# A three-phase sequence kernel on one core: start and middle reordered, and the first projections formed from high and low parts

## What is computed

```python
a = tanh(x @ WA.T); b = x @ WB.T                  # 16 states
h[t] = a[t] * h[t-1] + b[t]
g = sigmoid(x @ Wg.T + bg); dx = x @ WD.T + bD
x = layernorm(x + (h @ WC.T) * g + dx * (1 - g))
```

```python
w = x @ router_w + router_b;  topv, topi = top_k(w, 512)
sel = sort(topi[:, :511]);  x_sel, pos, w_sel, mask = rows of these tokens
hn = rmsnorm(x_sel, ln1)
q = rope(hn @ wq); k = rope(hn @ wk); v = hn @ wv     # 16 heads of 16
o = softmax(q k^T / 4 + mask) v @ wo;  x1 = x_sel + o
x2 = x1 + gelu(rmsnorm(x1, ln2) @ w1) @ w2
out = x with its chosen rows replaced by x2 * w_sel, other rows as they are; then layernorm(x + out)
```

## Time and profile before

| | |
|---|---|
| median of 3 runs | 514.93 us (514.45 to 515.61) |
| profiled execution | 513.3 us, of it span 511.4 us |
| busy in the span | PE 457.1, DVE 393.8, ACT 290.8, POOL 173.4 us |
| loop, 38 to 200 us | PE busy 149.65, DVE 137.21, ACT 84.44, POOL 104.42 of 162 us |
| passage, 240 to 256 us | PE 13.91, DVE 5.49, ACT 13.11 of 16 us |
| attention, 290 to 307 us | PE 17.00, DVE 16.51, ACT 15.86 of 17 us |

### The profile page before, as it was taken

One profiled execution on the slowest core, in us unless ns is written; L12 is line 12 of the kernel. 1 busy time (PEld: TensorE's weight loads), 2 busy tenths in 40 slices (PEclk: granted clock), 3 DMA queues, 4 the chain that ended last, 5 costly groups with the idle time before them and its releaser, 6 DMA issues.

```text
span 511.4 us, 10221 instructions
## 1 busy us (share of the span) xinstructions
PE 457.1 (89%) x3533; PEld 336.6 (66%) x3533; DVE 393.8 (77%) x1213; ACT 290.8 (57%) x614; POOL 173.4 (34%) x210
## 2 busy tenths in 40 slices
PE   7698999997999877998997999998998999998970
PEld 5587888776888633666674666665886666674860
DVE  4777898799788788787279999978667999966250
ACT  2435656553464532033888999954577999962200
POOL 9146667755775750373234000001000000000532
PEclk9899999999999999799999999998999999999995
DMA  8613342252222120167661000000000000000110
GB/s 244 221 43 84 107 141 83 82 155 94 83 83 83 42 84 0 39 200 240 210 191 30 3 2 3 2 2 1 0 1 2 2 1 2 3 2 1 35 37 11
DMA packets 29370, 33.89 MB, mean 66 GB/s; under 512 B 5860, under 2 KB 24968, under 8 KB 29320
## 3 DMA queue, kind: packets, MB, share of 16 engines
q1 hardware_dynamic: 23088, 24.78, 15.0%
q0 software_dynamic: 3520, 8.40, 5.5%
q10 hardware_dynamic: 2712, 0.06, 0.3%
HBM read 19.59 MB, written 13.63 MB: 65 GB/s over the span
## 4 chain that ended last, share of the span: by engine, by line
PE 46%; DVE 12%; POOL 9%; issue 7%; ACT 6%; POOLq 1%; DVEq 0%; ACTq 0%
PE ps L942 11%; PE ps L957 7%; PE ps L929 6%; PE ps L1032 4%; POOL arena L503 3%; PE ps L1009 3%; PE ps L879 3%; PE ps L666 2%; PE ps L898 2%; PE ps L781 2%; POOL r L512 2%; PE ps L905 1%; ACT arena L1252 1%; PE ps L1015 1%; POOL h_parts L562 1%
## 5 line engine op out<-in xcount | busy, mean ns | idle before, releaser
L1252 ACT ACTIVATE arena<-arena,nmax 128x511 f32<-128x511 f32 x128 | 91.5, 719 | 5.4 <-DVE nmax L1695 5.3
L1695 DVE CUSTOM_DVE_ANT_0 arena<-ps,nmask 128x511 f32<-128x511 f32 x128 | 84.8, 683 | 0.2 <-DVE nmask L1643 0.2
L942 PE MATMUL ps<-ident,arena 128*128 128x128 f32 x512 | 78.6, 276 | 3.7 <-ACT big L407 2.4
L942 PEld LDWEIGHTS ps<-ident,arena 128*128 128x128 f32 x512 | 58.7, 140 | 25.4 <-ACT arena L1252 15.0
L700 PE MATMUL ps<-wgd_hi,x_hi 128*128 128x512 f32 x128 | 51.9, 406 | 0.0
L702 PE MATMUL ps<-wgd_hi,x_lo 128*128 128x512 f32 x128 | 50.8, 397 | 0.0
L701 PE MATMUL ps<-wgd_lo,x_hi 128*128 128x512 f32 x128 | 50.6, 395 | 0.0
L929 PE MATMUL ps<-arena 96*128 96x512 bf16 x128 | 48.5, 385 | 1.9 <-DVE nmask L1643 1.1
L407 DVE COPY big<-ps 128x512 f32<-128x512 f32 x64 | 44.0, 688 | 5.0 <-PE ps L942 3.8
L503 POOL TENSOR_TENSOR arena<-arena 128x512 f32<-128x512 f32 x32 | 41.2, 1290 | 12.6 <-DVE arena L1360 11.1
L407 ACT COPY big<-ps 128x512 f32<-128x512 f32 x64 | 36.9, 576 | 8.3 <-PE ps L957 6.4
(11 more groups left out here) (250 smaller groups left out, 1041.3 us busy)
## 6 DMA issues: line engine op xcount, KB each, us to landing
arena<-in_L_attn_x SPq DMA_DIRECT2D x16, 512.0 KB, 4.6
out<-ob_sb SPq DMA_DIRECT2D x16, 512.0 KB, 3.2
w_sb<-in_L_ffn_w SPq DMA_DIRECT2D x2, 1024.0 KB, 10.7
mt_scratch<-nmask SPq DMA_DIRECT2D x8, 256.0 KB, 2.8
mt_scratch<-big SPq DMA_DIRECT2D x8, 256.0 KB, 4.6
big<-in_L_attn_Wg SPq DMA_DIRECT2D x1, 256.0 KB, 4.4
big<-in_L_attn_WD SPq DMA_DIRECT2D x1, 256.0 KB, 4.8
wqk<-in_L_ffn_wq SPq DMA_DIRECT2D x1, 256.0 KB, 7.7
```

The costliest lines, as they stand in the source:

```text
L942: mm = pe.transpose(ps[:, 2 + u % 2, k * P:(k + 1) * P], pr[u % 4][:, k * P:(k + 1) * P], ident[:, :])
L1252: act.activation(pr[u % 4][:, 0:K - 1], sm[u % 4][:, 0:K - 1], ACT.Exp, bias=nmax[:, c, h:h + 1], scale=-1.0, accum_out=rsum[:, c, h:h + 1 ...
L1695: dve.tensor_tensor_reduce(sm[u % 4][:, 0:K - 1], ps[:, S_BANKS[u % AHEAD], 0:K - 1], nmask[b][:, c, 0:K - 1], 1.0, 3.4e38, ALU.add, ALU.m ...
```

## The change

What it does, by parts:

- **Start.** PE begins with 9 fills of 512 columns on a zeroed tile as soon as that is there, and gets 12 more fills of 256 columns than before between its turns. POOL writes the constant hi_rep (an iota of 4096 elements) as its sixth step and no longer after the other constants. DVE makes wc_r before the first scan, and PE turns wc before the recurrence inputs and the second half of group 1 between group 0's input products and its state products.
- **Loop.** wq, wk and wv are multiplied by their gains in rounds 2 and 4 and rounded in rounds 3 and 5 on ACT; POOL subtracts the rounded from the full weights in rounds 4 and 6; `positions` moves from POOL's round 6 to 7.
- **Passage.** The copy of the turned x_sel is rounded (hnT_hi), DVE subtracts to get the rest (`rest_of_first`, first_lo), and each projection is made of three fp32r products instead of one f32 product. The picks of sequence 1 are made in one run of 32 products. DVE takes the odd mask tiles of sequence 1, and the mask's columns are turned one step earlier. The fills before `turn_split` are gone.
- **Attention 0** takes the banks in another order; ACT rounds w1 inside it, in turns 1 and 2.

```diff
@@ start @@
+            pe.wait_ge(bias_zeroed, 1)
+            zero_bits = bias_row.bitcast(BF16)
...
+            fill_zero(9)
             pe.wait_ge(ident_ready, 2)
...
+            fill_ident(8)
             transposes(0, 1)
+            fill_ident(4)
...
-            pe.wait_ge(split_ready, KD)
-            recurrence_inputs(0)
+            fill_ident(4)
             pe.wait_ge(split_ready, KD + 1)
...
+            recurrence_inputs(0)
+            transposes(1, 0)
             pe.wait_ge(split_ready, 2 * KD + 1)
             for G in range(NGB):
                 if G == 0:
-                    gates(G, 0)
+                    gate_inputs(G, 0)
+                    transposes(1, 1)
+                    state_products(G, 0)
@@ POOL, loop @@
+            def rest_of_weights(k):
+                pool.wait_ge(gain_ready, 2 * k + 3)
+                pool.tensor_tensor(wqk_lo[:, k, :], wqk[:, k, :], wqk_hi[:, k, :].bitcast(F32), ALU.subtract)
+                pool.tensor_tensor(wv_lo[:, k, :], wv_sb[:, k, :], wv_hi[:, k, :].bitcast(F32),
+                                   ALU.subtract).then_inc(w_lo_ready, 1)
+                pool.wait_ge(w_lo_ready, k + 1)
...
-                if G == 6:
+                if G in (4, 6):
+                    rest_of_weights(G // 2 - 2)
+                if G == 7:
                     positions()
@@ ACT, loop @@
                     gate(G, 1)
+                if G == 1:
+                    act.wait_ge(w2_loaded, 16 * (7 + 2 * HG))
+                    act.mul(q_gain[:, :], ln_col[:, 0, :], -(HD ** -0.5)).then_inc(gain_ready, 1)
+                    act.wait_ge(gain_ready, 1)
+                if G in (2, 4):
+                    scale_weights(G // 2 - 1)
+                if G in (3, 5):
+                    round_weights(G // 2 - 1)
@@ PE, passage @@
+            def project_high(b, c):
...
+                for o, hi, lo in outputs(c):
+                    for k in range(KD):
+                        for w in (hi, lo):
+                            pe.matmul(o, hnT_hi[:, k, c * P:(c + 1) * P], w[:, k, :],
+                                      start=(k == 0 and w is hi), stop=False)
+            def project_rest(b, c):
+                pe.wait_ge(hnT1_lo_ready, b * C + c + 1)
+                for (o, hi, _), signal in zip(outputs(c), (qk_done, v_done)):
+                    for k in range(KD):
+                        mm = pe.matmul(o, first_lo[:, k, c * P:(c + 1) * P], hi[:, k, :], start=False, stop=(k == KD - 1))
...
-            project(0, range(1))
+            project_high(0, 0)
+            pick_all(1)
+            project_rest(0, 0)
...
-            pe.wait_ge(v_ready[1], 2)
-            fill(7, 10)
@@ DVE, passage @@
-            angles(0)
             slots(1)
             one_hots(1)
+            rest_of_first(0, 0)
+            rest_of_first(0, 1)
+            factors(0)
+            angles(0)
+            rows(1)
...
+            odd_mask_rows()
             for c in range(C):
                 copy_turned(0, c)
                 if c < 2:
                     parts(0, 2 + c)
                     value(1, 2 + c)
-            copy_mask()
+                elif c == 2:
+                    copy_mask()
@@ ACT, attention 0 @@
+                        if b == 0 and u == 3 and hg in (1, 2):
+                            high_of_w1(hg - 1)
```

More of the change, by code:

```diff
@@ L55 @@
 AHEAD = 4
[L56 removed]
+S_BANKS = ((6, 7, 0, 1), (0, 1, 6, 7))
 M_BANKS = (4, 6, 5, 7)
[L58 removed]
 LAG = 7
@@ L747, in _ @@
             mm.then_inc(w_turned, 1)
-            for c in range(KD):
-                transposes(1, c)
+            recurrence_inputs(0)
+            transposes(1, 0)
             pe.wait_ge(split_ready, 2 * KD + 1)
@@ L893, in turn_split @@
                     pe.wait_ge(e_ready[n], done + 1)
-                for m in range(2):
+                for m in ((1, 0) if done == C - 1 else range(2)):
                     for half in range(2):
```

275 lines of the change are left out of this document (162 added, 113 removed).

## The result

The changed kernel takes 521.76 us (median of 4 runs, 520.86 to 523.77) against 514.69 us before (4 runs): the ratio is 1.0144, 95% interval 1.0106 to 1.0182. It is slower by 7 us, where I had forecast 515.2 and no difference. The time lies outside my range.

What follows compares the result with a forecast made beforehand. The prediction took a ring of ACT and DVE to bound the loop, a DVE chain the start. Its terms, 6.6 - 3.6 - 3.9 + 1.2 = +0.3 us, gave 515.2 us at the median, no difference, range 511.3 to 518.6.

Steps and rivals of the forecast that it cites:

- What bounds the loop: Loop: a ring of ACT and DVE, 9.44 us a turn, not PE; extra work costs some 80% of its length.
- part 1: Loop: gains, rounding and subtractions added on ACT and POOL cost +6.6 us, bounds 5.4 and 9.4.
- Rival A: Loop: the ring has slack, so the additions cost only about 2 us; 510.6 us in all, chance 0.15.
- Part 2, the start: Start: earlier iota and new order bring the state product near 15.8; -3.6 us, bounds -5.6 and -1.5.
- rival B: Start: cast held over the memsets and PE at half clock, so it gains about 1; 517.8 us, chance 0.13.
- Part 3, the passage: Passage: split and mask copy 2.4 us sooner each, less table load and clock; -3.9 us, bounds -5.5 and -0.5.
- the mask tiles of sequence 0 still start at 235.2, as before: Passage: no delay to sequence 0's mask tiles from the picks' wait, since angles(1) ends then either way.
- With four on DVE that is 2 us less on ACT before turn_split: Passage: dividing the mask tile copies takes 2 us off ACT; the split was to come 2.4 us sooner.
- copy_mask ... now it is before it: -2.4: Passage: the mask copy moved ahead of the last turned k gains 2.4 us, less 0.3 for ACT's table load.
- The clock, which I had at 0.6 at one place with even odds: Passage: PE may idle to half clock before the first split, up to 1.5 us late; 0.6 at even odds.
- Rival C: Passage: gains 1 only, as PE's half clock or the picks make the chunks late; 518.1 us, chance 0.13.
- Part 4: Attention 0: two casts of w1 on ACT in turns 1 and 2 cost +1.2 us, bounds 0 and 2.

Runs made afterwards that it cites:

- weights_after: The changed kernel with the weights' gains, rounding and POOL's subtraction moved behind the loop: 518.67 us, ratio 1.0101 to the kernel before.
- again: The changed kernel profiled a second time with nothing edited: 520.62 us (1 run).
- late_gather: The changed kernel, with POOL waiting for the fourth v of sequence 0 before gathering sequence 1's mask rows: 519.70 us (1 run).
- f32_order: The changed kernel's orders with the f32 products of before, weights and w1 prepared behind the loop: 509.20 us, ratio 0.9917 to the kernel before.
- f32_tiles_act: f32_order with ACT copying all mask tiles of sequence 1 and DVE none: 511.19 us, ratio 0.9942 to the kernel before.
- f32_mask_last: f32_order with the mask's columns turned and copied behind the last split, as before the change: 511.46 us, ratio 0.9963 to the kernel before.
- f32_cols_late: f32_order with POOL gathering sequence 1's mask columns only behind the last k copy: 511.24 us, ratio 0.9962 to the kernel before.
- fills: The changed kernel with fills where PE idled in the passage, among them 12 before sequence 1's picks: 517.78 us, ratio 1.0058 to the kernel before.
- f32_ kernels: f32_order and six variants of it, each with an edit to picks, mask tiles, column gathers, mask place or fills: 508.78 to 511.46 us.
- start_alone: The kernel before with the new start only; loop, passage and attention as before: 511.60 us, ratio 0.9951 to the kernel before.
- late_gather_timed: late_gather once more, timed: 517.65 us, ratio 1.0087 to the kernel before.

## Why the prediction was wrong

- **What bounds the loop, and part 1: right.** +6.6 was forecast, +6.6 and +6.3 measured, in the rounds named: 10.62, 10.26, 10.65, 10.70 and 10.25 us between the decays of groups 3 to 8. weights_after shows that these additions are the whole of it. (The upper bound of 9.4 adds to 8.9 by its own terms, which changes nothing.) Rival A is out. The sentence that ACT's time after the loop is free held for ACT alone: POOL's subtractions there cost 2.4 us of selection.
- **Part 2, the start: right in size, and that by luck.** -3.6 was forecast; -4.0 in most profiles, -2.4 to -2.8 in those that had half clock at 22 us. The first state product came at 17.88 us, not near 16: the cast of ident_b was held not until the iota ended at 6.2 but until 7.46, over the memsets behind it.

```profile
2.01 5.45 DVE L1409 CAST ident_b<-ident 128x128 bf16<-128x128 f32 x1 [2.01 <-POOL ident L472]
...
2.01 4.18 POOL L475 IOTA qk<- 128x4096 bf16 x1
6.15 0.97 POOL L478 MEMSET h_parts<- 128x512 f32 x2
```

  That is the mechanism of rival B. The chain that I had priced at -4.4 gave 2.3 to 2.5 us (20.21 to 17.88 and 17.70). The rest of the -4.0 is the clock: from the state product to the decays of group 1 it took 6.45 us before, 6.30 in the changed profile and 4.93 in again, where PE was at full clock. I had put that saving only into the better bound. So the size of this term came out by luck, from two errors of opposite sign.
- **Part 3, the passage: here it failed.** -3.9 was forecast, +4.6 to +6.1 measured. The step that failed with the most weight is "the mask tiles of sequence 0 still start at 235.2, as before": counted from the gather they start at 28.9 us and not at 24.07. Of these 4.8 us the gap at the last projection is 3.3 to 4.2 (late_gather). The rest, 0.6 to 1.6, is in every kernel with the new order that has no fills ahead of the picks, with f32 products too (25.41).
- The second step that failed is "With four on DVE that is 2 us less on ACT before turn_split", by which the split was to come 2.4 us sooner. From sequence 1's first tile to the split it takes 6.38 us before, 6.38 with the tiles divided (f32_order) and 6.38 with all on ACT (f32_tiles_act), and 9.25 and 8.13 in the changed kernel, where PE waits 2.5 us for DVE's first odd tile. I had walked through both streams with the durations of before, in which DVE comes to its tiles in time. f32_order's split is 0.3 us earlier than before, not 2.4.
- "copy_mask ... now it is before it: -2.4", less 0.3 for the table load, measured -1.35 in the changed kernel (6.13 and 4.78). That f32_mask_last gave 2.6 is in part luck: half of it is PE's clock. Taken together the orders of the passage were worth 0.7 us against the profile of before (+1.3, -1.7, +1.0 and -1.35 by parts), and 1.7 by the times; not 3.9.
- The clock, which I had at 0.6 at one place with even odds, cost 0.7 to 2.6 us in the mask tiles of the changed kernel, and in f32_order 1.5 in the projection of chunk 1. Rival C named the mechanism, but gave it a loss of 2.9 against the forecast; the miss was 8.5 to 10.
- What no rival held are the two gaps, waits of 3.6 and 2.1 us. Moving POOL's gathers removed each of them (late_gather, f32_cols_late), but POOL's gathers alone are not the cause. The first gap is absent in fills, where they were not moved, and in all seven f32_ kernels, whose last projection also runs beside the mask row gathers (ACT waits 1.89 us for PE there, released by PE). The second is in start_alone with the order of before. In the one profile that I had of before neither is to be seen, so I had no row from which to expect them. What makes them come and go stays open.
- That eight subtractions on DVE were "beside other work" is not so for the first two. They stand ahead of the angles, for which the picks wait, and the picks begin 10.0 to 10.1 us behind the gather (changed, again, weights_after, late_gather) instead of 9.12 with f32 products: 0.9 us.
- **Part 4: not shown.** +1.2 was forecast and +0.7 and +1.0 measured, but the stage varies by more than that without this edit, and no run takes the two casts out alone.

The sum of +0.3 came from terms ten times its size, so it was as uncertain as these. The passage's worse bound, -0.5, was still a gain, although the stage's order had been laid by hand and no part of the trace showed it: a schedule of that length should have had a loss among its bounds.

## What to carry to other kernels

Idle time inside a ring is no cover: read the period between two equal steps, and put additions outside it. When work is moved into time that looks idle on one engine, look at what its partner does there: POOL's elementwise work slows small DVE steps, by 2.4 us in this selection. A hand-laid order over several engines is only worth what the slowest branch lets through, so price each exchange by itself, from one fixed instant to the next and not by the whole stage: here one of two equal-looking exchanges gave 1.35 us in its own place and the other 0, and each changed PE's clock behind it, by some 1.5 us. Dropping the products while keeping the orders gave 509.2 us, better than both kernels. Profile the kernel before more than once: its passage showed no gap in the first profile, and one of 1.5 us and more in start_alone, where nothing in it was edited.

## What the runs showed of the hardware

- In three profiles with three products (changed, again, weights_after) ACT and DVE went on 2.5 to 3.5 us behind the ends of the products that they waited for, at PE's last projection of sequence 0. POOL issued a group of four indirect gathers then, and the profile names no releaser. With the gathers moved the wait was gone (2 profiles); with fills behind the projection it was gone with the gathers in place (1), and with f32 products it was never there (7). At the third split DVE waited 1.5 to 3.3 us beside the column gathers in eleven profiles, one of them with the order of before (start_alone), 0.8 in a twelfth (late_gather_timed), and 0.43 or nothing in the three with these gathers moved. But in the profile of before it waited 0.43 with the gathers in place.
- Thirty-two picks (60 columns, bf16) took 3.87 and 3.91 us at a granted clock of 0.50 and 0.58 (weights_after, changed) and 3.86 at 1.00 (fills), while 12 blocks of 128x128 f32 turned in 2.79 us at 0.50 and 1.50 at 1.00, and the 32 products of a split took 3.58 and 1.96.
- A DVE step over 15 elements took 0.99 us instead of 0.17 beside a POOL subtraction, and a cast of 128 columns took 5.45 us beside POOL's iota and memsets, where it took 1.30 before.
- The same start gave 22.6 to 22.8 us in twelve profiles and 23.9 to 24.3 in three. In the window from 22 to 24 us PE's granted clock was 1.00 (2.4 GHz) in the twelve, and 0.50, 0.53 and 0.67 in the three, so at 1.2 GHz for all or part of it.
